# Opening of a stack of four graph attention layers: layer norm's scale moved to scores and V, row sums on VectorE, score rows by transposes, idle matmuls 20, 3 and 3

## The chip, the cores and the metric

The kernel runs on one core of a Trainium2 chip. The metric is the device time of one execution in microseconds (us), median over runs. Five engines work side by side, each through its own instruction list in order: TensorE (PE in the profile, with its weight loads as PEld), VectorE (DVE), ScalarE (ACT), GpSimd (POOL) and SyncE (SP); they wait for each other by semaphores. TensorE reads SBUF and writes PSUM. An fp32 matmul stands in the profile as two instructions, a transpose as one.

## What is computed

`x` is 2048 x 128 fp32, `adj` a 2048 x 2048 matrix of 0 and 1, some 0.8% ones. Four residual layers:

```python
h = jnp.maximum(_layernorm(x, axis=-1), 0.0)
x = x + _L0_gnn_ref(h, adj, W_heads, a1, a2, W_out, b_out)   # 8 heads, ELU, projection
h = jnp.maximum(_layernorm(x, axis=-1), 0.0)
x = x + _L1_gnn_ref(h, adj, W, r)                            # 1 head, exact GELU
...                                                          # two more, 1 head, ELU
# one head:
Wh = h @ W; s1 = Wh @ a1; s2 = Wh @ a2
e = leaky_relu(s1[:, None] + s2[None, :], 0.2)
att = softmax(where(adj > 0, e, NEG), axis=1)
hp = att @ Wh                                                # a row without a neighbour: the mean of Wh
```

The layer norm has no weights: `(x - m) / sqrt(v + eps)`. With y = 1 / sqrt(v + eps), one number per row and positive, relu((x - m) * y) is relu(x - m) * y.

## The kernel before

**Tiling.** The 2048 rows are 16 tiles of 128. A unit is one head and one half (`c`, 1024 output rows, 8 groups of 128). For each of 16 tiles `j` of source rows, VectorE makes a `probs` tile of 128 x 1024 in one scalar_tensor_tensor (L1183; in the first two tiles two halves of 512, L1180) out of `rho`, the row factors spread over the partitions, `t_now`, a column factor, and `adjT`, the transposed adjacency as 0 or 1 in bf16. TensorE multiplies the 8 blocks of it with `V[:, j, :]`, which holds 128 columns of W h times a factor v, and v itself as column 129, so that the last column gives the softmax's denominator (L447 in layer 0, L472 later). `probs` is a ring of 8 tiles. Layer 0 has 16 units: `unit(0, 0)` outside the loop, then a loop of 7 rounds with two units each, then the late layers with parts of 8, 6 and 2 groups.

**Opening.** SyncE loads X in two halves, then weights, then `adj` tiles into 7 landing places (5 in `stage`, one in `hpT`, one in `xn`); ScalarE casts each to bf16 (`cast`, L699), and a place is loaded again once it has been cast. Before the 7th, SyncE waits for the first two transposed blocks (L314), as `xn` then holds normed rows. VectorE takes mean and variance (L1090, L1094); ScalarE takes the inverse root (L705, L707), VectorE improves it by one Newton step (L1098 to L1101); both norm the 16 tiles (L1105, L714); TensorE transposes them in four blocks of 512 columns (L367), both engines copy them to `hT` with relu (L1110, L719, the latter with sums of rows). TensorE makes W h of head 0 and the s2 of all 8 heads in one product per tile (`first_wh_and_s2`, L378, 136 columns), then s1 of head 0 as rows for the first 1024 nodes (`s1`, L383, 2 matmuls of 512 columns), and, between these two, spreads the largest score over the partitions (`first_spread_max`, L404). From it follow the factors (L739, L740), V of tile 0 on VectorE (L1134) and of the others on ScalarE (`first_scale_v`), and `rho` (L752).

**Beside unit 0.** TensorE does asides between tiles: after j=1 the maxima of all heads (L411) and s1 of 8 heads for nodes 1024 to 2047 (`rows_of_heads(1)`, 2 matmuls of 512 columns, so 4 instructions), after j=7 the same for nodes 0 to 1023, after j=11 the mean of W h (`mean_rows`, L426). VectorE does `center_of_heads` after j=3, `mean` after j=6 (L1157 to L1163), `add_bias` after j=12 (L1252). ScalarE casts, scales V and makes `rho_rows`, which go through DRAM to `rho`.

**Loop.** In the odd unit `project` makes W h of the next head (L395), ScalarE's `scale_v` makes V of it (L759, L761) with `v_now`. After j=7 VectorE takes the denominators of the unit before, after j=8 it divides, after j=10 it makes the ELU and its 32 x 32 transposes; ScalarE moves the blocks (L796), and TensorE projects at j=10 or 11 (`aside`, L571).

**Idle matmuls.** `keep_warm(count)` issues matmuls of the identity whose result nobody reads (L416): 20 at the start, 2 + 2 after the score vectors (L586), `WARM_ROWS` = 8 in the transition from layer 1 to 2 (`rest_of_scores(1)`, L636), and `WARM_HOLE` = 4 at the end of each of the three transitions (L663), before the products of `late_unit(n, 0)`.

Of the kernel before, what the change touches and what calls it, by code (L numbers as in the profile page):

```python
# [14 lines left out]
def gat_stack(nc, x, adj_t, w0, w0_t, a0, w_out, b_out, w1_t, w1, r1, w2, w2_t, av2, w3, w3_t, av3, out):  # L15
# [7 lines left out]
    P = 128  # L23
# [20 lines left out]
    with ctx:  # L44
# [21 lines left out]
        s2_all = sb("s2_all", [P, NT, H])  # L66
# [8 lines left out]
        wa0 = sb("wa0", [P, 2, H])  # L75
# [35 lines left out]
        CT, CC, CW = 264, 396, 480  # L111
        FT, FC = 140, 270
# [4 lines left out]
        first_xn = [xn, rows[:, 0, :, :]]  # L117
# [12 lines left out]
        first_norm_dve = sem("first_norm_dve")  # L130
        first_norm_act = sem("first_norm_act")
# [169 lines left out]
        def _(sp):  # L301
# [59 lines left out]
        def _(pe):  # L361
            def transpose_first(r):

                pe.wait_ge(first_norm_dve, r + 1)
                pe.wait_ge(first_norm_act, r + 1)
# [5 lines left out]
            def first_wh_and_s2():  # L371
# [3 lines left out]
                for t in range(NT):  # L375
                    if t % 4 == 0:
                        pe.wait_ge(first_hT_act if t % 8 else first_hT_dve, t // 8 + 1)
# [205 lines left out]
            keep_warm(WARM_START[0], idle_first)  # L583
            pe.wait_ge(w0t_in, 32)
            for h in range(H):
                last = nc.tensor.matmul(score_bank[:, CW + 2 * h:CW + 2 * h + 2], W0t[:, h, :], a0_sb[:, h, :],  # L586
                                        start=True, stop=True)
            last.then_inc(wa_psum, 1)
# [104 lines left out]
        def _(act):  # L693
# [15 lines left out]
            def first_transposed():  # L709
                act.wait_ge(rstd_ready, 1)  # L710
                for r in range(4):
                    for k in range(2, 4):
                        at = 4 * r + k
                        last = nc.scalar.activation(first_xn[r // 2][:, at % NK, :], X[:, at, :], ACT.Identity,  # L714
                                                    bias=nwt[:, 3, at:at + 1], scale=nwt[:, 0, at:at + 1])
                    last.then_inc(first_norm_act, 1)
                for r in (1, 3):
                    act.wait_ge(first_hT_psum, r + 1)
                    nc.scalar.activation(hT[:, r * 512:(r + 1) * 512], first_banks[r], ACT.Relu,  # L719
                                         accum_out=hsum[:, r:r + 1]).then_inc(first_hT_act, 1)  # L720

            def first_copy_wh(b):

                act.wait_ge(first_wh, b + 1)
                ins = nc.scalar.activation(V[:, PER_BANK * b:PER_BANK * (b + 1), 0:D],
# [902 lines left out]
```

## Time and profile before

| | us |
|---|---|
| median of 3 runs | 758.48 (758.44 to 759.07) |
| the profiled execution, its own time | 759.12 |
| its span, first to last instruction | 757.4 |
| TensorE busy | 746.5 (99%) |
| VectorE busy | 619.6 (82%) |
| ScalarE busy | 326.4 (43%) |

The page's second part cuts the span in 40 slices of 18.9 us and gives the busy share of each in tenths:

```profile
PE   8999999999999999999999999999999999999997
DVE  4989679797787968879796797968788969898986
DMA  9993000000000000000000000000000000000001
```

TensorE is busy from end to end, a little less in the first slice; the transfers of `adj` fill the first three. A time of an instruction runs from its start to its end, and neighbours overlap, so for a rate the text takes the distance from one start to the next, or the chain of waits, which cuts the overlap off.

### The profile page before, as it was taken

To read this page: it belongs to the slowest core of one execution; us is meant where nothing else is said; L and a number is where in the kernel's file an instruction comes from. 1 tells how busy PE (TensorE), PEld (TensorE's weight loads), DVE (VectorE), ACT (ScalarE), POOL (GpSimd) and SP (SyncE) were. 2 spreads that over 40 slices of the span, in tenths; PEclk is the share of its full clock that TensorE was granted. 3 is DMA by queue.
4 is the path that set the end of the run, shared out by engine and by line. 5 is a ranking of instruction groups with operands and counts; after the bars stand their busy time and mean duration, and the time that the engine had idled before them with its cause. 6 is when DMAs were issued, how large, how long until landed. Compare 5 with 4: busy or idle time off the path is not lost.

```text
span 757.4 us, 16076 instructions
## 1 busy us (share of the span) xinstructions
PE 746.5 (99%) x6507; PEld 732.4 (97%) x6507; DVE 619.6 (82%) x1048; ACT 326.4 (43%) x878; POOL 16.6 (2%) x38
## 2 busy tenths in 40 slices
PE   8999999999999999999999999999999999999997
PEld 8789999999999999999999999999989989998997
DVE  4989679797787968879796797968788969898986
ACT  4978341452543346134353414534350352636230
POOL 3000000000000000000000000000000000000000
PEclk9999999999999999999999999999999999999999
DMA  9993000000000000000000000000000000000001
GB/s 293 341 373 109 29 29 1 28 0 28 28 0 28 0 28 0 28 28 0 28 0 28 28 0 28 0 0 1 2 2 1 1 1 2 1 1 1 2 26 32
DMA packets 13874, 29.39 MB, mean 39 GB/s; under 512 B 1296, under 2 KB 7568, under 8 KB 13840
## 3 DMA queue, kind: packets, MB, share of 16 engines
q1 hardware_dynamic: 11152, 20.00, 7.8%
q0 software_dynamic: 2688, 8.92, 3.4%
q8 instruction: 24, 0.39, 0.2%
q14 instruction: 10, 0.08, 0.0%
HBM read 27.80 MB, written 1.11 MB: 38 GB/s over the span
## 4 chain that ended last, share of the span: by engine, by line
PE 95%; DVE 3%; ACT 1%; DMA 1%; issue 0%; DVEq 0%; ACTq 0%
PE acc L447 57%; PE acc L472 26%; PE side L571 3%; PE side L395 3%; PE acc L524 1%; PE acc L416 1%; PE side L383 1%; DMA X<-in_x_dram 1%; PE side L535 1%; PE acc L378 0%; PE side L511 0%; DVE stats L1090 0%; PE side L497 0%; PE side L426 0%; PE side L367 0%
## 5 line engine op out<-in xcount | busy, mean ns | idle before, releaser
L447 PE MATMUL acc<-V,probs 128*128 128x129 f32 x3840 | 436.6, 275 | 1.5 <-DVE probs L1180 1.5
L447 PEld LDWEIGHTS acc<-V,probs 128*128 128x128 f32 x3840 | 432.6, 192 | 4.5 <-DVE V L1134 2.3
L1183 DVE SCALAR_TENSOR_TENSOR probs<-rho,t_now,adjT 128x1024 f32<-128x1024 f32 x238 | 290.0, 1277 | 13.9 <-PE acc L447 9.1
L1273 DVE SCALAR_TENSOR_TENSOR probs<-rho,t_now,adjT 128x768 f32<-128x768 f32 (+3 forms) x182 | 147.3, 868 | 13.3 <-PE acc L472 10.5
L796 ACT ACTIVATE hpT<-rows 32x256 f32<-32x256 f32 x224 | 92.8, 414 | 66.6 <-DVE rows L1220 64.2
L472 PE MATMUL acc<-stage,probs 128*128 128x129 f32 x1024 | 115.9, 275 | 0.0
L472 PEld LDWEIGHTS acc<-stage,probs 128*128 128x128 f32 x1024 | 115.0, 192 | 0.1
L472 PE MATMUL acc<-V,probs 128*128 128x129 f32 x768 | 89.4, 275 | 0.0
L472 PEld LDWEIGHTS acc<-V,probs 128*128 128x128 f32 x768 | 87.4, 192 | 0.1
L781 ACT ACTIVATE fill<-mean_now,empty 128x128 f32<-128x128 f32 x120 | 36.7, 396 | 89.8 <-DVE den L1196 89.8
L1228 DVE TENSOR_TENSOR X<-X,side 128x512 f32<-128x512 f32 x28 | 19.3, 688 | 65.9 <-PE side L571 65.9
L759 ACT ACTIVATE V<-v_now 128x4 f32<-128x4 f32 x28 | 5.9, 209 | 83.0 <-PE side L395 83.0
L761 ACT ACTIVATE V<-side,v_now 128x128 f32<-128x128 f32 x112 | 31.5, 363 | 0.0
L1205 DVE SCALAR_TENSOR_TENSOR rows<-acc,den,fill 128x128 f32<-128x128 f32 x112 | 30.8, 343 | 0.3
L395 PE MATMUL side<-W,hT 128*128 x224 | 29.6, 275 | 0.0
L571 PE MATMUL side<-Wout,hpT 128*128 x224 | 27.3, 275 | 0.0
L395 PEld LDWEIGHTS side<-W,hT 128*128 128x128 f32 x224 | 27.3, 192 | 0.0
L571 PEld LDWEIGHTS side<-Wout,hpT 128*128 128x128 f32 x224 | 26.1, 192 | 0.0
L893 ACT ACTIVATE rows<-acc,late_den 128x128 f32<-128x128 f32 x32 | 11.0, 394 | 30.5 <-DVE late_den L1311 26.3
L699 ACT ACTIVATE adjT<-stage 128x1024 bf16<-128x1024 int32 x24 | 23.8, 1043 | 0.0
L788 ACT ACTIVATE rows<-rows 128x512 f32<-128x512 f32 x28 | 17.5, 629 | 10.3 <-DVE rows L1205 10.2
L918 ACT ACTIVATE xn<-X,nwt 128x128 f32<-128x128 f32 x36 | 14.7, 482 | 16.6 <-DVE nwt L1415 16.6
(207 smaller groups left out, 406.5 us busy)
## 6 DMA issues: line engine op xcount, KB each, us to landing
stage<-in_adj_t_dram SPq DMA_DIRECT2D x24, 512.0 KB, 7.1
rho<-rho_dram POOLq DMA_DIRECT2D x15, 512.0 KB, 3.9
hpT<-in_adj_t_dram SPq DMA_DIRECT2D x4, 512.0 KB, 8.5
xn<-in_adj_t_dram SPq DMA_DIRECT2D x4, 512.0 KB, 7.2
X<-in_x_dram SPq DMA_DIRECT2D x2, 512.0 KB, 4.6
W0t<-in_W_t_dram SPq DMA_DIRECT2D x1, 512.0 KB, 5.2
W<-in_L_gnn_W_heads_dram SPq DMA_DIRECT2D x1, 512.0 KB, 6.5
Wout<-in_L_gnn_W_out_dram POOLq DMA_DIRECT2D x1, 512.0 KB, 10.2
```

The costliest lines, as they stand in the source:

```text
L395: last = nc.tensor.matmul(side[:, g % 2, k * D:(k + 1) * D], hT[:, j * P:(j + 1) * P], w, start=True, stop=True)
L447: last = nc.tensor.matmul(group(c, k), probs[:, j % RING, k * P:(k + 1) * P], V[:, j, :], start=(j == 0 and k % PER_BANK == 0), stop=(j == ...
L472: last = nc.tensor.matmul(group(c, k), slot_of(n, p, j)[:, i * P:(i + 1) * P], v[:, j, :], start=(j == 0 and k % PER_BANK == 0), stop=(j = ...
L571: last = nc.tensor.matmul(side[:, b, k * D:(k + 1) * D], hpT[:, 4 * b + k, :], w, start=True, stop=True)
L699: nc.scalar.activation(adjT[:, j, c * CH:(c + 1) * CH], landing(n), ACT.Sign).then_inc(adj_ready, 1)
L761: last = nc.scalar.activation(V[:, 4 * g + k, 0:D], side[:, g % 2, k * D:(k + 1) * D], ACT.Copy, scale=v_now[:, 4 * g + k:4 * g + k + 1])
L781: ins = nc.scalar.activation(fill[:, k, :], mean_now[:, :], ACT.Copy, scale=empty[:, c, k:k + 1])
L796: last = nc.scalar.activation(hpT[b:b + Q, :, a:a + Q], rows[a:a + Q, 1, :, b:b + Q], ACT.Copy)
L1183: nc.vector.scalar_tensor_tensor(probs[:, j % RING, :], rho[:, c * CH:(c + 1) * CH], t_now[:, j:j + 1], adjT[:, j, c * CH:(c + 1) * CH], A ...
L1205: ins = nc.vector.scalar_tensor_tensor(rows[:, 0, k, :], group(c, k)[:, 0:D], den[:, 3, k:k + 1], fill[:, k, :], ALU.mult, ALU.add)
L1228: nc.vector.tensor_tensor(at, at, side[:, b, :].rearrange("p (k d) -> p k d", k=4), ALU.add).then_inc(x_added, 1)
L1273: return nc.vector.scalar_tensor_tensor(slot_of(n, p, j)[:, first:end], rho[:, at + first:at + end], t_now[:, j:j + 1], adjT[:, j, at + fi ...
```

## The change

The centred rows relu(x - m) take the place of the normed ones. The scale y is put on later: on the scores as they leave PSUM (`first_scores_of`), and on V through `vy_now` and `vy_all`, v times y, while column 129 keeps v. So the first half is centred by ScalarE as soon as its means are there, the second by VectorE, and root and Newton step run behind the transposes. `W0s` is 144 columns wide and gives s1 of all heads too, by node in the partitions; rows of head 0 come from 8 matmuls of 128 columns against the identity, rows of all heads from 8 transposes per half. The sum of the rows of h is made on VectorE in unit 0 (`scale_of_rows` after j=5 and j=6 in place, `sum_of_rows` after j=7), a matmul with minus one brings it to the partitions, and ScalarE scales it. Score vectors are made in two groups of four heads with the first transposes between. The idle matmuls of 2 + 2 go, 8 become 3, 4 become 3. SyncE no longer waits ahead of the 7th load.

```diff
-    WARM_START, WARM_ROWS, WARM_HOLE = (20, 2), 8, 4
+    WARM_START, WARM_ROWS, WARM_HOLE = 20, 3, 3
-    MW = D + H
+    MW = D + 2 * H
...
-                elif n == SLOTS - 1:
-                    sp.wait_ge(first_hT_psum, 2)
...
-            def s1(k, wa_s1, bank):
-                nc.tensor.matmul(bank[0:wa_s1.shape[1], :], wa_s1, hT[:, k * 512:(k + 1) * 512],
-                                 start=True, stop=True).then_inc(s1_psum, 1)
+            def s1_of_first(tiles):
+
+                for t in tiles:
+                    last = nc.tensor.matmul(side[:, t // 4, (t % 4) * P:(t % 4 + 1) * P], s1_all[:, t, 0:1].to_broadcast([P, P]), ident[:, :],
+                                            start=True, stop=True)
+                if tiles[-1] % 4 == 3:
+                    last.then_inc(s1_psum, 1)
...
+            score_vectors(range(0, H // 2))
+            transpose_first(0)
+            score_vectors(range(H // 2, H))
+            for r in range(1, 4):
+                transpose_first(r)
...
-            keep_warm(WARM_START[1], idle_first)
-            wa1 = wa0[:, 0, :]
-            wa_head = wa0[:, 0, 0:1].to_broadcast([P, P])
-            keep_warm(WARM_START[1], idle_first)
-            for r in range(4):
-                transpose_first(r)
             first_wh_and_s2()
-            s1(0, wa_head, side[:, 0, :])
+            pe.wait_ge(scores_ready, 1)
+            s1_of_first((0, 1, 2, 3))
             first_spread_max()
-            s1(1, wa_head, side[:, 1, :])
+            s1_of_first((4, 5, 6, 7))
+            def sum_of_first():
+                pe.wait_ge(h_sum_ready, 1)
+                pe.wait_ge(rho_ready, 6)
+                nc.tensor.matmul(side[:, 0, 0:1], h_sum[:, :], minus_one[:, 0:1], start=True, stop=True).then_inc(h_sum_psum, 1)
 
             def rows_of_heads(c):
                 pe.wait_ge(rho_ready, 4 - 2 * c)
                 for k in range(2):
-                    s1(2 * c + k, wa1, side[:, k, :])
+                    for i in range(4):
+                        last = nc.tensor.transpose(side[0:H, k, i * P:(i + 1) * P], s1_all[:, 4 * (2 * c + k) + i, :], ident[:, :])
+                    last.then_inc(s1_psum, 1)
 
             unit(0, 0, 0, ((1, spread_max_of_heads), (1, lambda: rows_of_heads(1)), (7, lambda: rows_of_heads(0)),
-                           (11, lambda: mean_rows(1, W0[:, :, :].rearrange("p h d -> p (h d)"), H, rho_ready, 6)),
+                           (10, sum_of_first), (12, lambda: mean_rows(1, W0[:, :, :].rearrange("p h d -> p (h d)"), H, rho_ready, 6)),
                            ))
...
+            def first_centered():
+                act.wait_ge(neg_mean_ready, 1)
+                for t in range(NK):
+                    last = nc.scalar.activation(first_xn[0][:, t, :], X[:, t, :], ACT.Relu, bias=neg_mean[:, t:t + 1])
+                    if t % 4 == 3:
+                        last.then_inc(first_norm_act, 1)
...
+                nc.scalar.activation(vy_now[:, :], vy_all[:, bass.ds(h + 1, 1), :].rearrange("p a t -> p (a t)"),
+                                     ACT.Copy).then_inc(tv_ready, 1)
+                act.wait_ge(tv_ready, 2 * h + 4)
...
             nc.scalar.preload_act_table_set(LOG_EXP)
-            first_inverse_root()
+            first_centered()
+            first_transposed(0)
             act.wait_ge(wa_psum, 1)
             wa_scores = score_bank[:, CW:CW + 2 * H].rearrange("p (h s) -> p s h", s=2)
-            nc.scalar.activation(W0s[:, D:MW], wa_scores[:, 1, :], ACT.Copy)
-            nc.scalar.activation(wa0[:, :, :], wa_scores, ACT.Copy).then_inc(wa_ready, 1)
-            first_transposed()
+            nc.scalar.activation(W0s[:, D:D + H], wa_scores[:, 1, :], ACT.Copy)
+            nc.scalar.activation(W0s[:, D + H:MW], wa_scores[:, 0, :], ACT.Copy).then_inc(wa_ready, 1)
+            first_transposed(1)
+            first_inverse_root()
+            cast(0, 2)
             for b in range(NB):
-                if b < 2:
-                    cast(b, b + 1)
                 first_copy_wh(b)
-            cast(2, 3)
...
-            cast(15, 20)
+            cast(15, 17)
+            act.wait_ge(h_sum_psum, 1)
+            nc.scalar.activation(hmean[:, 1:2], side[:, 0, 0:1], ACT.Copy, scale=-1.0 / N).then_inc(hmean_ready, 1)
+            cast(17, 22)
...
+            def first_scores_of(t0, t1, raw):
+
+                y = nwt[:, 0, t0:t1]
+                to = scores_all[:, t0:t1, :]
...
+                    return nc.vector.tensor_tensor(to, raw, y, ALU.mult)
...
+                dve.wait_ge(first_vexp, 1)
+                nc.vector.tensor_tensor(vy_now[:, :], V[:, :, D], nwt[:, 0, :], ALU.mult).then_inc(first_vy, 1)
+                dve.wait_ge(first_vy, 1)
                 dve.wait_ge(first_copied, 1)
-                dve.wait_ge(first_vexp, 1)
-                nc.vector.tensor_scalar(V[:, 0, 0:D], V[:, 0, 0:D], V[:, 0, D:D + 1], None, ALU.mult).then_inc(first_v, 1)
+                nc.vector.tensor_scalar(V[:, 0, 0:D], V[:, 0, 0:D], vy_now[:, 0:1], None, ALU.mult).then_inc(first_v, 1)
...
+            def scale_of_rows(c):
+
+                own = first_xn[c]
+                y = nwt[:, 0, c * NK:(c + 1) * NK].rearrange("p (k d) -> p k d", d=1).to_broadcast([P, NK, D])
+                last = nc.vector.tensor_tensor(own, own, y, ALU.mult)
+                if c == 1:
+                    link(last)
+
+            def sum_of_rows():
+
+                nc.vector.tensor_reduce(h_sum[:, :], rows[:, :, :, :].rearrange("p c k d -> p d (c k)"), AX.X, ALU.add).then_inc(h_sum_ready, 1)
...
+            unit(0, 0, rho_and_adj(0, 0, True), ((3, center_of_heads), (5, lambda: scale_of_rows(0)), (6, lambda: scale_of_rows(1)),
+                                                     (7, sum_of_rows), (8, scale_of_heads), (12, add_bias)))
```

## Rows read from the trace of the kernel before

**Rows 1.** The page, part 1: busy us (share of the span) and instructions.

```profile
PE 746.5 (99%) x6507; PEld 732.4 (97%) x6507; DVE 619.6 (82%) x1048; ACT 326.4 (43%) x878; POOL 16.6 (2%) x38
```

**Rows 2.** The chain of waits, 0 to 60 us: start us, us, what.

```profile
7.20 1.53 DVE stats L1090 x8
...
13.82 1.71 PE acc L367 x8
15.53 3.78 PE acc L378 x32
19.31 0.86 PE side L383 x2
...
20.20 0.50 PE acc L404 x2
...
23.16 3.81 PE acc L447 x32
...
27.28 1.81 PE side L383 x4
```

**Rows 3.** The timeline of the opening: start us, us, engine, line, what.

```profile
8.81 1.95 PE L586 MATMUL acc<-a_sb,W0t 128*128 128x2 f32 x16 [0.71 <-DMA W0t<-in_W_t_dram]
...
22.06 0.29 DVE L1134 TENSOR_SCALAR V<-V 128x128 f32<-128x128 f32 x1 [0.49 <-ACT V L739]
22.26 2.74 DVE L1180 SCALAR_TENSOR_TENSOR probs<-rho,t_now,adjT 128x512 f32<-128x512 f32 x4
```

**Rows 4.** TensorE in stretches: A:B length, busy (count), granted clock, DMA share, GB/s.

```profile
8.73:12.14 3.41, 3.13 (x26) 1.00 1.10 367
12.14:15.55 3.41, 3.41 (x18) 0.50 1.04 356
...
18.96:22.37 3.41, 2.66 (x10) 1.00 1.03 382
```

**Rows 5.** VectorE's groups by shape: count, busy us, mean ns, idle before.

```profile
L1252 DVE TENSOR_TENSOR X<-X,bias_rep 128x2048 f32<-128x2048 f32 x1 | 2.3, 2284 | 0.0
...
L1427 DVE TENSOR_SCALAR xn<-X,mv 128x128 f32<-128x128 f32 x6 | 1.4, 283 | 0.1
...
L1457 DVE TENSOR_REDUCE neg_c<-acc 128x1 f32<-128x128 f32 x3 | 0.9, 291 | 1.5 <-PE acc L559 1.5
...
L1123 DVE TENSOR_REDUCE cmax<-s_all 128x8 f32<-128x128 f32 x1 | 0.4, 383 | 0.0
```

**Rows 6.** The timeline of units 0 and 1.

```profile
31.41 1.21 DVE L1157 TENSOR_REDUCE hsum<-hT 128x2 f32<-128x1024 f32 x1
...
32.92 3.67 DVE L1183 SCALAR_TENSOR_TENSOR probs<-rho,t_now,adjT 128x1024 f32<-128x1024 f32 x3
...
58.14 1.29 DVE L1183 SCALAR_TENSOR_TENSOR probs<-rho,t_now,adjT 128x1024 f32<-128x1024 f32 x1 [0.57 <-PE acc L447]
...
69.74 6.81 ACT L796 ACTIVATE hpT<-rows 32x256 f32<-32x256 f32 x16 [0.46 <-DVE rows L1220]
...
79.31 1.95 PE L571 MATMUL side<-Wout,hpT 128*128 x16
```

**Rows 7.** The chain of waits in the transition to layer 2.

```profile
546.56 1.88 PE acc L416 x16
...
548.66 0.44 PE side L511 x4
```

**Rows 8.** The timeline of the same transition.

```profile
546.60 1.26 ACT L918 ACTIVATE xn<-X,nwt 128x128 f32<-128x128 f32 x3
...
547.01 0.42 DVE L1342 SCALAR_TENSOR_TENSOR rows<-rows 128x256 f32<-128x256 f32 x1
...
556.06 3.93 DVE L1273 SCALAR_TENSOR_TENSOR probs<-rho,t_now,adjT 128x512 f32<-128x512 f32 x5 [0.42 <-ACT rho L959]
...
556.96 3.25 PE L472 MATMUL acc<-stage,probs 128*128 128x129 f32 x27
```

**Rows 9.** Waits of all engines: us in total, times, longest.

```profile
ACT V L759 <- PE side L395: 83.0, 28, 7.7
```

More of the change, by code:

```diff
@@ L116, in gat_stack @@
         first_banks = [side[:, 0, :], side[:, 1, :], acc[:, 1, 0, :], acc[:, 1, 1, :]]
-        first_xn = [xn, rows[:, 0, :, :]]
+        first_xn = [rows[:, 1, :, :], rows[:, 0, :, :]]
+        s2_all, s1_all = scores_all[:, :, 0:H], scores_all[:, :, H:2 * H]
         spare_bank, max_bank = acc[:, 0, 2, 0:2 * P], acc[:, 0, 2, 2 * P:3 * P]
@@ L362, in transpose_first @@
             def transpose_first(r):
-                pe.wait_ge(first_norm_dve, r + 1)
-                pe.wait_ge(first_norm_act, r + 1)
+                if r < 2:
+                    pe.wait_ge(first_norm_act, r + 1)
+                else:
+                    pe.wait_ge(first_norm_dve, r - 1)
                 for k in range(4):
@@ L582, in _, with score_vectors @@
             pe.wait_ge(ident_ready, 1)
-            keep_warm(WARM_START[0], idle_first)
+            keep_warm(WARM_START, idle_first)
             pe.wait_ge(w0t_in, 32)
[L585 to L588, printed above, removed]
+            def score_vectors(heads):
+                for h in heads:
+                    last = nc.tensor.matmul(score_bank[:, CW + 2 * h:CW + 2 * h + 2], W0t[:, h, :], a0_sb[:, h, :],
+                                            start=True, stop=True)
+                if heads[-1] == H - 1:
+                    last.then_inc(wa_psum, 1)
+            score_vectors(range(0, H // 2))
[3 more added lines that the diff above has]
+                transpose_first(r)
             def later_vectors():
@@ L707, in first_inverse_root, with first_transposed @@
                 nc.scalar.activation(nwt[:, 0, :], nwt[:, 2, :], ACT.Exp, scale=-0.5).then_inc(root_ready, 1)
[L709 to L720, printed above, removed]
+            def first_centered():
[4 more added lines that the diff above has]
+                        last.then_inc(first_norm_act, 1)
+            def first_transposed(r):
+                act.wait_ge(first_hT_psum, r + 1)
+                nc.scalar.activation(hT[:, r * 512:(r + 1) * 512], first_banks[r], ACT.Copy).then_inc(first_hT_act, 1)
             def first_copy_wh(b):
                 act.wait_ge(first_wh, b + 1)
+                act.wait_ge(scores_ready, 1)
                 ins = nc.scalar.activation(V[:, PER_BANK * b:PER_BANK * (b + 1), 0:D],
@@ L732, in first_scale_v @@
                     where = V[:, t, 0:D] if t < NK + 1 else first_group(t)[:, 0:D]
-                    last = nc.scalar.activation(V[:, t, 0:D], where, ACT.Copy, scale=V[:, t, D:D + 1])
+                    last = nc.scalar.activation(V[:, t, 0:D], where, ACT.Copy, scale=vy_now[:, t:t + 1])
                 last.then_inc(v_ready, 1)
@@ L829, in _ @@
             act.wait_ge(first_copied, NB)
-            act.wait_ge(first_vexp, 1)
+            act.wait_ge(first_vy, 1)
             first_scale_v(0)
-            cast(3, 6)
+            cast(2, 5)
             first_scale_v(1)
-            cast(6, 8)
+            cast(5, 8)
             factors()
@@ L1087, in first_norm @@
                 for c in range(2):
+                    own = slice(c * NK, (c + 1) * NK)
                     dve.wait_ge(x_in[c], 16)
@@ L1091, in first_norm @@
                     link(last)
-                    nc.vector.memset(nwt[:, 1, c * NK:(c + 1) * NK], 0.0)
                     for k in range(c * NK, (c + 1) * NK):
                         last = nc.vector.bn_aggr(mv[:, k, :], stats[:, k, :])
+                    if c == 0:
+                        link(last)
+                        nc.vector.tensor_scalar(neg_mean[:, :], mv[:, own, 0], -1.0, None, ALU.mult).then_inc(neg_mean_ready, 1)
                 last.then_inc(var_ready, 1)
-                y, s, m = (nwt[:, i, :] for i in (0, 1, 3))
+                dve.wait_ge(var_ready, 1)
+                for t in range(NK, NT):
+                    last = nc.vector.tensor_scalar(first_xn[1][:, t - NK, :], X[:, t, :], mv[:, t, 0:1], 0.0, ALU.subtract, ALU.max)
+                    if t % 4 == 3:
+                        last.then_inc(first_norm_dve, 1)
+                for r in (2, 3):
+                    dve.wait_ge(first_hT_psum, r + 1)
+                    nc.vector.tensor_copy(hT[:, r * 512:(r + 1) * 512], first_banks[r]).then_inc(first_hT_dve, 1)
+                y, s = (nwt[:, i, :] for i in (0, 1))
                 dve.wait_ge(root_ready, 1)
@@ L1140, in center_of_heads, with scale_of_heads @@
                 dve.wait_ge(rows_ready, 1)
-                s2 = s2_all[:, :, :].rearrange("p t h -> p h t")
+                s2 = s2_all.rearrange("p t h -> p h t")
                 nc.vector.tensor_tensor(d_all[:, :, :], s2, c_rep[:, :].rearrange("p (h t) -> p h t", t=1)
                                         .to_broadcast([P, H, NT]), ALU.subtract).then_inc(d_ready, 1)
+            def scale_of_rows(c):
[3 more added lines that the diff above has]
+                if c == 1:
+                    link(last)
+            def sum_of_rows():
+                nc.vector.tensor_reduce(h_sum[:, :], rows[:, :, :, :].rearrange("p c k d -> p d (c k)"), AX.X, ALU.add).then_inc(h_sum_ready, 1)
+            def scale_of_heads():
+                dve.wait_ge(tv_ready, 2)
+                nc.vector.tensor_tensor(vy_all[:, :, :], v_all[:, :, :], nwt[:, 0, :].rearrange("p (h t) -> p h t", h=1)
+                                        .to_broadcast([P, H, NT]), ALU.mult).then_inc(vy_all_ready, 1)
             def last_columns(to, c):
@@ L1254, in add_bias @@
                 dve.wait_ge(x_added, 1)
-            unit(0, 0, rho_and_adj(0, 0, True), ((3, center_of_heads), (6, lambda: mean(0, 1)), (12, add_bias)))
+            unit(0, 0, rho_and_adj(0, 0, True), ((3, center_of_heads), (5, lambda: scale_of_rows(0)), (6, lambda: scale_of_rows(1)),
+                                                     (7, sum_of_rows), (8, scale_of_heads), (12, add_bias)))
             dve.wait_ge(tv_ready, 2)
```

71 lines of the change are left out of this document (32 added, 39 removed).

## The prediction

> **What bounds the kernel now.** I read the page first: TensorE is busy for 746.5 of 757.4 us [rows 1]. So a change pays only where it takes instructions off TensorE, or where TensorE waits, and that is in the first 23 us and in the three transitions between late layers. Second, the chain of waits over the opening [rows 2]: it goes over VectorE's statistics, the transposes, 32 products of W h and s2 that end at 19.31, the spread of the maximum at 20.20, and the products of unit 0 from 23.16. From there it stays on TensorE, with `rows_of_heads` (1.81) inside. Third, the timeline of the opening [rows 3] and TensorE's granted clock [rows 4]: it is 0.50, the lower level of 1.2 GHz, from 12.14 to 15.55, after a stretch in which TensorE did 16 products of two columns, 8 idle matmuls and one or two transposes. Everything here is worked against the profiled execution, span 757.4, own time 759.12; that is 0.6 above the median of 758.48, and differences are taken over to the median as they are.
>
> **Opening, up to the products' end.** Removed: the wait of both norms for root and Newton step. Centring needs the means alone. Those of the first half are there when VectorE goes on to the second half, 7.20 [rows 2]; with a small negation and its links ScalarE starts at about 7.5. The nearest row for one step is 1.26 for three with scale and bias [rows 8], 0.42 each, so eight end by 10.9. VectorE begins its eight at about 9.7; the same form takes at most 0.283 [rows 5], so they end by 12.0. TensorE's score vectors start at 8.81 and take 1.95 [rows 3], four heads 0.98. Its list then: heads to 9.8, first block of transposes (0.44 at the high clock [rows 7]) to 10.2, heads to 11.2, second and third block to 12.1. Each finds its rows ready, by 0.2 us or more. The fourth block and the 32 products of W h follow. These widen from 136 to 144 columns: 3.78 / 32 = 0.118 [rows 2] becomes 0.125, altogether 0.2 more.
>
> Their clock is the open question. If it falls at 12.1 and comes back at 15.5, as before, a transpose costs 1.71 / 8 = 0.214 [rows 2] and a product 0.214 x 144 / 128 = 0.24. The fourth block ends at 12.9, eleven of the 32 run until 15.55, and the other 21 take 2.6: end at 18.2, 1.1 before the old 19.31. If it doesn't fall: 12.5 + 32 x 0.125 = 16.5, 2.8 before. I take the first. In the same stretch before, the idle matmuls gave 8 of 128 columns; the change gives 12 transposes and the same small products, and it drops the idle ones. That is little more than what let it fall.
>
> The Trainium skill, TensorE: Matmul & The Clock Gate, "Part 4: PE-mode transpose", says that transposes don't count as busy for the clock as matmuls do. The trace speaks against it, as the stretch from 12.14 to 15.55 held transposes almost alone and the clock rose at its end [rows 2, 4]. By that rule the case without a fall would be impossible, and the time that of the first case.
>
> **Opening, up to the first product.** From the end of the 32 to the spread it was 0.89 (19.31 to 20.20) with TensorE's s1 beside it (0.86) [rows 2]. Now the two last scaled reads and the same reduction stand there, and 8 instructions of 128 columns, 8 x 0.11 = 0.9: unchanged. The three copies to V (`first_copy_wh`), for which the spread waits, have the casts of two tiles before them; they end ahead of it in both cases. From the spread to the first product it was 2.96. Added: the product v times y on VectorE ahead of V of tile 0, with a wait on itself; the start-to-start distance of a small one is 0.20 [rows 3]. Queued behind it are V of tile 0 and the first probs half, for which TensorE waits. So +0.2, bounds 0.15 and 0.35. Root, Newton step and the two casts run behind transposes and W h: nothing. The opening gives 1.1 - 0.2 = 0.9.
>
> SyncE's removed wait starts the 7th load 5 us sooner, but the transfers are already at a share of 1.04 and more [rows 4] and land in turn: nothing. The cast of tile 2 moves behind the first scaling of V; VectorE wants it after four halves, 2.7 us [rows 3], and it is there after some 2.4. Cover 0.3 us, and TensorE doesn't want it before another 2 us.
>
> **Score rows.** 4 instructions in 1.81 [rows 2] become 8 transposes of 0.11, 0.9, twice: 1.8 to 1.9 off a busy TensorE. Their sum costs two instructions, 0.2 (bounds 0.1 and 0.4). Net 1.7.
>
> **VectorE in unit 0.** Each `scale_of_rows` is a tensor_tensor of 1024 elements: half of 2.28 [rows 5], with the fixed part 1.2; both 2.4. `scale_of_heads` adds 0.4. Removed are the old reductions, 31.41 to 32.92 [rows 6], 1.5. The reduction of 2048 elements reads them 512 bytes apart. No row shows that. Lower bound: contiguous, 2.28 [rows 5]. Above: 128 scores read 32 bytes apart took 0.383, 128 contiguous ones 0.291 [rows 5], so 0.72 ns more an element, 2.28 + 1.5 = 3.8. I take 3.8, the strided row being the nearer one.
>
> Who waits: probs tile 8 was ready at 32.92 + 2 x 1.22 = 35.4 [rows 6]; now 35.4 + 2.4 - 1.5 + 3.8 = 40.1. TensorE took it at 27.28 + 1.81 + 96 x 0.113 + 1.81 = 41.7 [rows 2], now 39.8. So 0.3 of waiting; with 2.28, none. The second place is the projection of unit 1. VectorE's tile 23 started at 58.14, and the moved blocks were ready 18.4 later at 76.55, TensorE projected at 79.31 [rows 6]. By its own work VectorE would reach tile 23 at 32.92 + 16 x 1.21 + 2.3 (bias) = 54.6; with 2.4 - 1.5 + 3.8 + 0.4 it is 59.7, and the blocks are ready at 78.1. TensorE comes at 79.31 - 1.7 + 0.3 = 77.9. So 0.2 more. Cost 0.4, bounds 0 and 0.6.
>
> ScalarE's row mean now waits for TensorE's sum, with 15 casts behind it. Its list is two casts past the last `rho_rows`, before the sum; the scaled mean is there some 3 us before `mean_rows`, which moved to j=12. Nothing; a late cast of tile 15 or 16 would put TensorE on wait from 3 us on. In the loop ScalarE makes one more copy of 16 columns per head, before `scale_v`; it waits there for TensorE 83.0 us over 28 times [rows 9]: nothing.
>
> **Idle matmuls.** Of `WARM_ROWS` 16 instructions took 1.88 [rows 7]; six take 0.7. What is late next is the norm: ScalarE's three end at 547.86, VectorE's ELU at 547.43 [rows 8]. So the four transposes start at about 548.0 and not 548.66 [rows 7], and ScalarE's and VectorE's chain behind them moves along: 0.65, bounds 0.4 and 0.8. `WARM_HOLE` gives nothing: the product starts 0.90 after the first probs half (556.06, 556.96 [rows 8]), exactly as in the opening, 22.26 to 23.16 [rows 2, 3], where no idle matmul stands between. So probs set it.
>
> **Sum.** 0.9 + 1.7 - 0.4 + 0.65 = 2.85, say 2.8: median 758.48 - 2.8 = 755.7, a span of 754.6.
>
> **Rivals.**
> - B, the clock stays high at 12.1: the 32 end at 16.5 and not 18.2, 1.7 more. 754.0. For it: more transposes in that stretch than before, and they seem to count. Against it: the idle matmuls are gone.
> - C, it falls as before and once more when the products of unit 0 start. From 18.96 to 22.37 TensorE was busy for 2.66 with four instructions of 512 columns among ten [rows 4]. Now this stretch holds some 1.3 us of 128 columns, not far above the one that let it fall. A stretch of 3.4 us at half rate costs 1.7: 757.4.
> - D, the other sign: the reduction over 512 bytes a step is dearer than the 32-byte row tells. TensorE's loss is its length less 3.4; the rest of the change gives 3.2. Slower by more than 1.5 from 8.1 us on, 4 ns an element; at 9 us it is 5.6 lost, 760.9. Against it: the row gives 1.9 ns an element.
> - E, the score rows are no cheaper: 8 stationary loads of other data in a row cost the 0.214 of the low clock each, and 1.8 goes: 757.5. Against it: 0.44 for four transposes [rows 7].
>
> **How the numbers follow.** 0.2% is about what a measurement of this kernel can tell from no change: 757.0 and 760.0 are the bounds. The likeliest case A has 42% (own range 755.0 to 756.6), B 27%, C 20%, D 5%, E 4%, anything else 2%. Faster by over 0.2%: nearly all of A and B and a quarter of C, 72%. Within: most of C, E and a rest of A, 22%. Slower: D and a rest, 6%. The range takes in B with its bounds and C: 753.6 to 757.8.
>
> **What would show it.** In the new trace: the 32 products end at 18.2 (A, C) or 16.5 (B); first probs product at 22.3 or 20.6; the granted clock 0.50 around 12 to 15.5 and, in C, after 22; the two groups of 8 transposes 0.9 each; `sum_of_rows` 3.8 (2.3, or above 8); one wait of TensorE of 0.3 at tile 8; TensorE at the four transposes after the shortened idle ones 0.65 sooner relative to its neighbours; `WARM_HOLE`'s product 0.90 after its probs. What would make it wrong: a ScalarE centring above 0.5 each, so that TensorE waits at the second block, or a clock that falls elsewhere.

## The result, and the profile after

| | before | changed |
|---|---|---|
| median, us | 758.48 (758.43 to 759.07, 5 runs) | 754.37 (754.28 to 755.99, 5 runs) |
| ratio | | 0.9947, 95% interval 0.9936 to 0.9959 |
| profiled execution, its span | 759.12, 757.4 | 754.51, 752.8 |

The changed kernel is 4.1 us faster, 0.5%. The forecast was 755.7 in a range of 753.6 to 757.8. What came is the rival B: TensorE's clock did not fall in the opening. Below, a "fall" is a stretch in which the granted clock is at its lower level, 0.50 (1.2 GHz), after it had been at 1.00 (2.4 GHz); the "mean clock" of an execution is its granted clock averaged over the whole span, so that a fall shows in it as 0.998 or less.

The page of the changed kernel, part 1:

```profile
PE 742.0 (99%) x6505; PEld 731.8 (97%) x6505; DVE 624.3 (83%) x1048; ACT 326.6 (43%) x884; POOL 16.6 (2%) x38
```

TensorE has 4.5 us less of busy time than in [rows 1], VectorE 4.7 more. The chain of waits of the changed kernel, 0 to 60 us (start, us, what), is to be set beside [rows 2]:

```profile
11.78 0.87 PE acc L377 x8
12.65 3.92 PE acc L388 x32
16.57 0.89 PE side L395 x8
...
17.46 0.50 PE acc L418 x2
...
37.46 5.60 PE acc L461 x48
43.06 0.12 PE side L627 x2
...
46.85 1.72 PE side L440 x4
```

The transposes (L377) take 0.11 each (0.87 for eight, before 1.71). The 32 products (L388; by count of instructions, they are 16 products of two each) end at 16.57, and the spread (L418) starts at 17.46 and not 20.20. The stretches of the same kernel, TensorE alone (A:B, length, busy, granted clock, DMA share, GB/s), to be set beside [rows 4]:

```profile
8.73:12.14 3.41, 3.41 (x34) 1.00 1.10 361
12.14:15.55 3.41, 3.41 (x30) 1.00 1.04 355
...
18.96:22.37 3.41, 1.82 (x16) 1.00 1.01 378
```

The granted clock is 1.00, the upper level, where it was 0.50. The timeline of units 0 and 1:

```profile
20.55 3.81 PE L461 MATMUL acc<-V,probs 128*128 128x129 f32 x32 [1.60 <-DVE probs L1230]
...
24.61 1.04 PE L633 MATMUL side<-ident,scores_all 128*8 128x128 f32 x8
...
32.38 3.75 DVE L1196 TENSOR_REDUCE h_sum<-rows 128x128 f32<-128x2048 f32 x1
...
37.46 5.60 PE L461 MATMUL acc<-V,probs 128*128 128x129 f32 x48 [0.22 <-DVE probs L1233]
```

The first product starts at 20.55 (before 23.16). The eight transposes that make score rows take 1.04, the end of the last one included, and VectorE's reduction 3.75. TensorE waits 0.22 for probs tile 8. The projection of unit 1 stands in the chain as

```profile
75.37 1.99 PE side L585 x16
```

In the transition to layer 2 the chain of waits reads:

```profile
538.71 2.23 PE acc L486 x20
540.95 0.88 PE acc L549 x2
...
543.68 0.41 PE acc L503 x2
544.11 0.63 PE side L525 x4
...
549.37 0.49 PE acc L573 x2
```

The shortened idle group (`WARM_ROWS`) is off this chain altogether: the transposes (L503) wait for VectorE's ELU now, which ends at 543.54, and those of L525 stand behind them.

### The profile page after: what moved, and what is told of

The parts are those of the page before. It is cut to its first block, busy times and chain, and to the rows that moved or that the text cites. A ratio compares the mean times of both kernels' runs of the same rounds, so it can differ in the third digit from the quotient of the medians.

```text
span 752.8 us, 16085 instructions
## 1 busy us (share of the span) xinstructions
PE 742.0 (99%) x6505; PEld 731.8 (97%) x6505; DVE 624.3 (83%) x1048; ACT 326.6 (43%) x884; POOL 16.6 (2%) x38
## 4 chain that ended last, share of the span: by engine, by line
PE 94%; ACT 3%; DVE 2%; issue 1%; POOL 0%; POOLq 0%; DVEq 0%
PE acc L461 55%; PE acc L486 26%; PE side L585 3%; PE side L409 3%; ACT adjT L723 1%; PE acc L430 1%; PE acc L538 1%; ACT V L756 1%; PE acc L388 1%; PE side L549 1%; PE side L525 0%; PE side L511 0%; PE side L440 0%; DVE stats L1431 0%; ACT xn L947 0%
## 5 line engine op out<-in xcount | busy, mean ns | idle before, releaser
L461 PE MATMUL acc<-V,probs 128*128 128x129 f32 x3840 | 436.7, 275 | 1.8 <-DVE probs L1230 1.6
L461 PEld LDWEIGHTS acc<-V,probs 128*128 128x128 f32 x3840 | 432.6, 192 | 2.7 <-DVE V L1175 1.8
L486 PE MATMUL acc<-stage,probs 128*128 128x129 f32 x1024 | 115.9, 275 | 0.2
L486 PEld LDWEIGHTS acc<-stage,probs 128*128 128x128 f32 x1024 | 115.0, 192 | 0.6 <-issue 0.6
L486 PE MATMUL acc<-V,probs 128*128 128x129 f32 x768 | 89.4, 275 | 0.1
L486 PEld LDWEIGHTS acc<-V,probs 128*128 128x128 f32 x768 | 87.4, 192 | 0.3 <-issue 0.3
L784 ACT ACTIVATE V<-side,vy_now 128x128 f32<-128x128 f32 x112 | 31.5, 363 | 0.0
```

The source lines that it names most:

```text
L461: last = nc.tensor.matmul(group(c, k), probs[:, j % RING, k * P:(k + 1) * P], V[:, j, :], start=(j == 0 and k % PER_BANK == 0), stop=(j == ...
L486: last = nc.tensor.matmul(group(c, k), slot_of(n, p, j)[:, i * P:(i + 1) * P], v[:, j, :], start=(j == 0 and k % PER_BANK == 0), stop=(j = ...
L784: last = nc.scalar.activation(V[:, 4 * g + k, 0:D], side[:, g % 2, k * D:(k + 1) * D], ACT.Copy, scale=vy_now[:, 4 * g + k:4 * g + k + 1])
```

## Experiments

The line numbers of the changed kernel: products of the units L461 and L486, transposes of the opening L377, the 32 products L388, the spread L418, the spread of layer 2 L573, idle matmuls L430, the rows of all heads L633. All differences between kernels below are of medians, and within the traces of starts in the chain of waits.

**a_same: the changed kernel again.** No edit.

> The changed kernel once more, to see in how many executions the clock falls in the opening and what it costs: expected one in five with a mean clock of 0.996 to 0.998, 1.6 to 1.8 us above the others, which lie at 754.3 to 754.6. A rival by which the difference of the two levels is not the clock would show the levels without a difference in the clock.

The times are 754.17 to 754.28 in five runs, the mean clock 0.999 or 1.0 in each; ratio to before 0.9940 (0.9926 to 0.9953). None had a fall, so the longer time of a fall didn't show here. It did in the first five (755.99 at a mean clock of 0.996; the others 754.28 to 754.51 at 0.999 or 1.0), and in the next run.

**a_idle_8_4: idle matmuls of the late transitions back.**

```diff
-    WARM_START, WARM_ROWS, WARM_HOLE = 20, 3, 3
+    WARM_START, WARM_ROWS, WARM_HOLE = 20, 8, 4
```

> The changed kernel with the idle matmuls of the late transitions back at 8 and 4. Theory: 0.65 to 0.8 us more at the transition to layer 2, where the transposes wait behind them, and nothing at the other two, where the probs set the start: 755.1. Rival 1: the fourth one of the three transitions counts too, 0.22 each, 755.7. Rival 2: fewer idle matmuls cost clock, so putting them back gains: under 754.3.

The median is 755.02, 0.65 to 0.8 above the changed kernel's 754.37 and 754.23. One of its four executions had a fall; the other three, at 754.79, 754.94 and 755.10, are 0.6 to 0.7 above. By the chain, the transition from the products' end to the spread:

```profile
542.43 1.72 PE acc L549 x4
544.15 1.88 PE acc L430 x16
...
551.53 0.49 PE acc L573 x2
```

From the first to the last of these starts it is 9.10; in the changed kernel, from 540.95 to 549.37, 8.42. The 16 idle instructions are on the chain again, and the difference of 0.68 is all of it. At the end of the transition the timeline shows the start of the first probs half and of the product:

```profile
553.65 2.74 DVE L1324 SCALAR_TENSOR_TENSOR probs<-rho,t_now,adjT 128x512 f32<-128x512 f32 x4 [0.42 <-ACT rho L988]
...
554.54 1.69 PE L486 MATMUL acc<-stage,probs 128*128 128x129 f32 x13
```

They are 0.89 apart with four idle ones and 0.90 with three (551.48 and 552.38), so the fourth is free. Both rivals are refuted.

Its profiled execution, 756.72, is one in which the clock fell in the opening, and the instructions of the opening are those of the changed kernel. The stretch and the chain:

```profile
11.80:15.20 3.40, 3.40 (x17) 0.52 1.04 354
```

```profile
11.75 1.69 PE acc L377 x8
13.43 4.78 PE acc L388 x32
...
19.10 0.50 PE acc L418 x2
```

That is case A: the 32 products end at 18.21, and the spread is at 19.10, 1.64 after the changed kernel's 17.46. So one and the same opening runs either way.

**a_start10: ten idle matmuls fewer at the start.**

```diff
-    WARM_START, WARM_ROWS, WARM_HOLE = 20, 3, 3
+    WARM_START, WARM_ROWS, WARM_HOLE = 10, 3, 3
```

> The changed kernel with 10 and not 20 idle matmuls at the start. Theory (the clock carries the opening): TensorE has nothing from about 6 us until the weights land at 8.8, the granted clock falls or stays low through score vectors, transposes and part of the 32 products, and the first product of unit 0 comes 1.5 to 3 us later, 756 to 757.5. Rival (the order of the work carries it, the clock is a small matter): the idle matmuls reached past the landing at 8.9, so without them the opening is 0.3 sooner, 754.1.

The median is 758.69 (757.25 to 759.14, 10 runs): the whole gain is gone by ten matmuls that nobody reads. Stretches and chain of its profile:

```profile
8.80:12.00 3.20, 3.20 (x17) 0.50 1.09 365
12.00:16.00 4.00, 4.00 (x20) 0.50 1.05 358
16.00:20.00 4.00, 4.00 (x23) 0.65 1.02 347
```

```profile
8.62 1.87 PE acc L602 x8
...
13.89 1.71 PE acc L377 x8
15.60 5.57 PE acc L388 x32
```

TensorE idles for 2.8 us ahead of the weights. Then score vectors, transposes and some 13 of the 32 products run at the low level (the 32 take 5.57 and not 3.92, at 0.12 more for each that is slow), and the first product comes at 25.15, 4.6 later. In this profile the theory holds, and its 1.5 to 3 us were too few: I had not counted the score vectors (1.87 and 1.5 for 0.79 twice) and had the clock back too soon. The ten executions are not all of this kind: five have a mean clock of 0.992 or 0.993 (758.7 to 759.1), three 0.995 (757.3 to 757.5), and two have 0.999 and still take 758.5 and 758.7. No profile of such a one was kept, so what made those two long is open.

**b_idle_12 and b_idle_0: the kernel before with more and with no idle matmuls ahead of its transposes.**

```diff
-    WARM_START, WARM_ROWS, WARM_HOLE = (20, 2), 8, 4
+    WARM_START, WARM_ROWS, WARM_HOLE = (20, 6), 8, 4
```

> The kernel before with 6 + 6 and not 2 + 2 idle matmuls between score vectors and transposes, 1.8 us more of work that nobody reads, of which 0.2 lies in a wait. Theory (where the clock falls, the transposes and some products pay for it): no execution has the low clock at the transposes, mean clock 0.999 or 1.0 in all of them; against the executions that kept the clock it is 1.6 slower, 760.0, against those in which it fell 1.0 slower. Rival (idle work is free there, since norms and not TensorE set the transposes): 758.4.

The median is 758.84 against 758.55 of before beside it. Eight of ten executions kept the clock (758.70 to 758.97), two did not (760.3 and 760.4). So 1.8 us more of idle work cost 0.4 against those of before that kept it (758.31 to 758.67), not 1.6. Both expectations are wrong, mine by taking TensorE to be on the path there for all of it. Against the profile of b_same below, in which the norms hold the transposes, the last transposes end at 15.26 and not 14.89 and the first product comes at 22.89 and not 22.51: of the 1.8, the 0.4 by which the idle work reaches past the norms.

```diff
-    WARM_START, WARM_ROWS, WARM_HOLE = (20, 2), 8, 4
+    WARM_START, WARM_ROWS, WARM_HOLE = (20, 0), 8, 4
```

> The kernel before without the 2 + 2 idle matmuls. Theory: TensorE waits for the norms there, so no time by itself; but with less work ahead of the transposes the clock falls in more executions, so more of them at the upper of the two levels 758.4 and 759.1, and perhaps a longer low clock. Rival (these idle matmuls are without effect): half the executions at either level, as before.

The median is 759.23: one execution of ten kept the clock (758.39), four are at 758.9 to 759.0 and five at 759.4 to 759.7. Its profile, one of the five, has the 32 products in 4.62 and the spread at 20.74. The idle matmuls that the change drops did serve the clock of the kernel before, in which 31 of 48 executions kept it.

**b_same: the kernel before, a second profile.**

> The kernel before once more, for a second profile. If its clock stays high in the opening (expected in 6 of 10), its transposes take 0.9 and not 1.7 to 1.9 per eight, but the spread of the maximum is only 0.6 sooner than 20.2, since the last normed rows of ScalarE (14.1) hold the fourth block either way. A rival, by which the two levels 758.4 and 759.0 lie elsewhere in the kernel, would show the spread at 20.2 and the 0.6 later on.

This execution took 758.48, with the clock kept. Its timeline:

```profile
12.46 1.65 ACT L714 ACTIVATE rows<-X,nwt 128x128 f32<-128x128 f32 x4
...
13.44 0.42 PEld L367 LDWEIGHTS acc<-ident,rows 128*128 128x128 f32 x4 [0.34 <-DVE rows L1105]
13.47 1.40 PE L367 MATMUL acc<-ident,rows 128*128 128x128 f32 x8
...
19.55 0.49 PE L404 MATMUL acc<-ident_neg,cmax 128*128 128x128 f32 x2
```

The last eight transposes take 1.40, not 0.87, with 0.34 of waiting for rows between, and ScalarE's last normed row ends at 14.1. The spread is at 19.55, 0.65 before 20.20, and the first product at 22.51 and not 23.16. So in the kernel before the norms cover most of a fall: it costs 0.6. Further down its chain stand `mean_rows` in unit 0, which ends at 50.24, and the transition to layer 2:

```profile
48.52 1.72 PE side L426 x4
...
541.97 2.23 PE acc L472 x20
...
553.30 0.49 PE acc L559 x2
```

In the 48 runs of before beside the experiments, 17 have a mean clock of 0.997 and, but for one at 760.2, lie at 758.8 to 759.2; the others have 0.999 or 1.0 and lie at 758.2 to 758.8.

**a_root_first: the root ahead of the centring.**

```diff
             nc.scalar.preload_act_table_set(LOG_EXP)
+            first_inverse_root()
             first_centered()
             first_transposed(0)
...
             first_transposed(1)
-            first_inverse_root()
```

> The changed kernel with ScalarE's inverse root ahead of its centring again, so that the first half's rows wait for the variances of both halves, as the norm did before, 9.6 us and not 7.4. Theory (the early centring is what feeds TensorE through the opening): the first block of transposes comes at about 11.8 and not 9.9, the spread of the maximum 1.9 to 2.2 us later than 17.4, and where the clock falls in the wait some more; 756.2 to 757.5. Rival (the order of TensorE's list and the removed scale are the gain, ScalarE has time): within 0.5 of 754.3.

The median is 757.61 (755.9 to 759.26, 10 runs), and the times stand in three groups: three executions at 755.9 (mean clock 1.0), four at 757.6 to 757.7 (0.996 to 0.998), three at 759.2 to 759.3 (0.994). The profile is of the first group; timeline and chain:

```profile
11.32 0.66 PE L377 MATMUL side<-ident,rows 128*128 128x128 f32 x4 [1.33 <-ACT rows L736]
```

```profile
18.94 0.50 PE acc L418 x2
```

TensorE waits 1.33 for the rows, and the spread is 1.5 late where 1.9 to 2.2 were expected. 755.9 is 1.6 above the changed kernel, so the rival is refuted. The groups are 1.7 and 1.6 apart, about what one fall costs, and the lower mean clocks fit one and two falls. No profile of the second or third group was kept, so where in the kernel they lie is not shown, and they don't show rival C.

**a_rows_mm: the score rows by products again.**

```diff
-                    for i in range(4):
-                        last = nc.tensor.transpose(side[0:H, k, i * P:(i + 1) * P], s1_all[:, 4 * (2 * c + k) + i, :], ident[:, :])
-                    last.then_inc(s1_psum, 1)
+                    nc.tensor.matmul(side[0:H, k, :], W0s[:, D + H:MW], hT[:, (2 * c + k) * 512:(2 * c + k + 1) * 512],
+                                     start=True, stop=True).then_inc(s1_psum, 1)
```

> The changed kernel with one part undone: the score rows of all heads come from two products of 512 columns per half again and not from 8 transposes (they are taken without the layer norm's scale, so the values of the rows differ). Theory (TensorE is busy there, so its instructions are paid in full): 4 instructions of 0.45 in place of 8 of 0.11 at either place, 0.9 to 0.95 more each, 1.8 to 1.9 us in all, 756.2. Rival (eight stationary loads of other data cost as much as the wide products): within 0.3 us of the changed kernel, 754.4.

The median is 755.77, 1.4 to 1.5 above the changed kernel where 1.8 to 1.9 were expected, ratio to before 0.9960. The chain:

```profile
20.31 3.81 PE acc L461 x32
...
24.44 1.81 PE side L632 x4
26.25 10.92 PE acc L461 x96
```

The four instructions take 1.81 in place of 0.97, and again 1.81 in place of 0.87 at the second place (both in a_contig's chain, where TensorE doesn't wait either): 0.84 and 0.94, 1.8 in all. The products behind them start slower too: the 96 behind the first place take 10.92 and not 10.72, the 48 behind the second 5.56 and not 5.36, which is 0.4 more. At the first place it sits in the first seven, which take 0.98; the first seven of a_contig take 0.78. From the first product to the end of `mean_rows` it is 29.74 against a_contig's 27.56, so the score rows are worth 2.2, and the medians of these two runs are 2.1 apart. The changed kernel shows only 1.4 to 1.5 of it, because there TensorE waits for VectorE at tile 8 and at the projection of unit 1; with the dearer score rows it comes later and waits at neither (the projection takes 1.79 and not 1.99). The two are one account: the transposes give 2.2, and VectorE takes 0.7 of it back.

**a_contig: the reduction over neighbours.**

```diff
-                nc.vector.tensor_reduce(h_sum[:, :], rows[:, :, :, :].rearrange("p c k d -> p d (c k)"), AX.X, ALU.add).then_inc(h_sum_ready, 1)
+                nc.vector.tensor_reduce(h_sum[:, :], rows[:, :, :, :].rearrange("p c k d -> p (c k d)").rearrange("p (a b) -> p a b", b=2 * NK), AX.X, ALU.add).then_inc(h_sum_ready, 1)
```

> The changed kernel with the reduction of h reading its 2048 elements one behind the other and not 512 bytes apart (so it sums other elements than the rows' sum; the mean row is not the reference's). Theory (the distance is what makes it 3.75 us, and its length makes TensorE wait at probs tile 8 and at the projection of unit 1): 2.2 to 2.4 us, both waits of 0.2 gone, 754.0. Rival (128 results instead of one make it long): 3.75 as before and 754.4.

The median is 753.65, 0.6 to 0.7 below the changed kernel. The sum of other elements is a wrong mean row, so this kernel is only for measuring. Its timeline and its chain:

```profile
32.49 2.28 DVE L1196 TENSOR_REDUCE h_sum<-rows 128x128 f32<-128x2048 f32 x1
...
34.68 1.27 DVE L1233 SCALAR_TENSOR_TENSOR probs<-rho,t_now,adjT 128x1024 f32<-128x1024 f32 x1
```

```profile
25.75 10.72 PE acc L461 x96
36.47 0.87 PE side L633 x8
37.35 5.36 PE acc L461 x48
...
75.02 1.79 PE side L585 x16
```

The reduction takes 2.28 with the same 128 results, so the distance between elements makes the other 1.47. It is also what tile 8 waits for: the chain of the changed kernel names ScalarE's cast, which ends at 36.03 beside the reduction, but here `probs` of tile 8 starts at 34.68, before that cast ends (36.13). The three tiles from tile 8 on take 5.36 on the chain and not 5.60. From the first product (20.66) to the end of `mean_rows` (48.22) it is 27.56, in the changed kernel 28.02, and the projection itself is 1.79 and not 1.99: 0.46 + 0.2 = 0.66.

**best: the sum by halves, V of tile 0 by two factors.**

```diff
-                nc.vector.tensor_tensor(vy_now[:, :], V[:, :, D], nwt[:, 0, :], ALU.mult).then_inc(first_vy, 1)
-                dve.wait_ge(first_vy, 1)
                 dve.wait_ge(first_copied, 1)
-                nc.vector.tensor_scalar(V[:, 0, 0:D], V[:, 0, 0:D], vy_now[:, 0:1], None, ALU.mult).then_inc(first_v, 1)
+                nc.vector.tensor_scalar(V[:, 0, 0:D], V[:, 0, 0:D], V[:, 0, D:D + 1], nwt[:, 0, 0:1], ALU.mult, ALU.mult).then_inc(first_v, 1)
+                nc.vector.tensor_tensor(vy_now[:, :], V[:, :, D], nwt[:, 0, :], ALU.mult).then_inc(first_vy, 1)
...
-                nc.vector.tensor_reduce(h_sum[:, :], rows[:, :, :, :].rearrange("p c k d -> p d (c k)"), AX.X, ALU.add).then_inc(h_sum_ready, 1)
+                link(nc.vector.tensor_tensor(rows[:, 0, :, :], rows[:, 0, :, :], rows[:, 1, :, :], ALU.add))
+                link(nc.vector.tensor_tensor(rows[:, 0, 0:4, :], rows[:, 0, 0:4, :], rows[:, 0, 4:8, :], ALU.add))
+                link(nc.vector.tensor_tensor(rows[:, 0, 0:2, :], rows[:, 0, 0:2, :], rows[:, 0, 2:4, :], ALU.add))
+                nc.vector.tensor_tensor(h_sum[:, :], rows[:, 0, 0, :], rows[:, 0, 1, :], ALU.add).then_inc(h_sum_ready, 1)
```

> The changed kernel with two mends. The row sum is made by four additions of halves (1024, 512, 256 and 128 elements, all neighbours) and not by one reduction over 512 bytes a step; and V of tile 0 takes both factors, v and y, in one instruction, with their product for the other tiles behind it. Theory: VectorE's 3.75 us become 1.2 + 0.7 + 0.4 + 0.3 = 2.6, both waits of TensorE of 0.2 (probs tile 8, projection of unit 1) go with what hangs on them, 0.7 in all as with the reduction over neighbours, and the first product comes 0.2 sooner: 753.5. Rival (the three added waits of VectorE on itself and a slower two-factor form eat it): 754.0 or more.

The median is 753.79 (753.64 to 755.03, 5 runs), ratio to before 0.9937 (0.9924 to 0.9951), against 754.23 of the changed kernel beside it. It is 0.4 faster, and the four executions with the clock kept (753.64 to 753.85) lie below all of the changed kernel's. From the first product to the projection of unit 1 it has a_contig's 54.36. The second mend gave little. Timeline of VectorE:

```profile
19.11 0.34 DVE L1173 TENSOR_SCALAR V<-V,nwt 128x128 f32<-128x128 f32 x1 [0.42 <-ACT V L762]
19.37 0.17 DVE L1174 TENSOR_TENSOR vy_now<-V,nwt 128x16 f32<-128x16 f32 x1
19.46 2.73 DVE L1232 SCALAR_TENSOR_TENSOR probs<-rho,t_now,adjT 128x512 f32<-128x512 f32 x4
```

From the spread to the first product it is 3.02 (17.33 to 20.35) and was 3.09. The small product (L1174) still stands ahead of the probs, and V now takes 0.26 from start to start. So the second mend gave 0.07 and not 0.2.

## Why the prediction was right, and where it wasn't

The mechanisms held, the case that I held likeliest did not come, and the rival that did gave 754.0 for 754.37. The range held because it was made to take in that rival; the number 755.7 itself was the wrong case.

**The clock, the step that failed.** "I take the first" was wrong in three ways. First, how often: with this opening it fell in 3 of 28 executions (the changed kernel, a_same, a_idle_8_4, a_rows_mm, a_contig, best), in the kernel before in 17 of 48. Second, the reason I gave: that 12 transposes in place of 8 instructions of idle matmuls were little more than what let it fall. It was enough to keep the clock in most executions. Third, I compared a forecast with a fall to a median without one. The profiled 759.12 is an execution with a fall; the median is not. With a fall on both sides the change gives 759.0 - 756.0 = 3.0 (I had 2.8), without one 758.4 - 754.3 = 4.1. The difference is the finding of this case: before, the norms covered most of a fall, now TensorE alone sets the opening up to the spread, and a fall costs 1.64 by the traces (1.3 to 1.8 by the times) where it cost 0.6. The 1.7 of the forecast is right for the changed kernel. Rival B's 754.0 has the same flaw: its 4.5 is worked against the profile with a fall, and there it holds (spans 757.4 to 752.8, 4.6), but the median before is 0.6 lower.

Why the clock falls in one execution of a kernel and not in another is not shown. The moment at which the instructions first become fast differs: the 40 idle instructions at the start took 6.46 in the first profile of before and 7.42 in the second, 7.57 in the changed kernel's. Where they end early, TensorE waits for the weights. It waited 1.05 in a_idle_8_4, the only profile of this opening with a fall, and 0.71 (a_same), 0.27 (a_rows_mm), 0.16 (best) or not at all (the changed kernel, a_contig) in those without. One profile with a fall is a hint and no proof, and a_root_first waited 1.33 for its rows and kept the clock. That the work ahead of the stretch matters is shown by b_idle_0, b_idle_12 and a_start10; a_root_first, where that work stands behind a wait, points the same way by its mean clocks.

**Transposes and the clock.** [rows 2, 4] spoke against the rule of the Trainium skill, TensorE: Matmul & The Clock Gate, "Part 4: PE-mode transpose", that transposes don't count as busy for the clock. Case B, which has no place under that rule, came in 25 of 28 executions, with transposes where the idle matmuls had been; with neither ahead of it, in b_idle_0, the clock fell in nine of ten.

**Opening.** The working for B said 16.5 for the end of the 32 products and 20.6 for the first product; the trace has 16.57 and 20.55. For A it said 18.2 and, for the spread, 19.1; a_idle_8_4 has 18.21 and 19.10. The stretch from the spread to the first product grew from 2.96 to 3.09, by 0.13 where I had 0.2. The landing of the weights and the later rise moved the start of the score vectors between 8.7 and 9.3 in the profiles, a term I didn't have. Without a fall on either side the opening gave 22.51 - 20.55 = 1.96. That the early centring carries most of it is shown by a_root_first, 1.5 at the spread; the rest, with the new order of TensorE's list and of the casts, no run takes apart.

**Score rows.** The forecast counted the instructions alone, 1.8 to 1.9, and those gave 1.8; rival E is refuted. With the 0.4 at the start of the products behind them they are worth 2.2; why these start slower is not shown. The sum cost 0.12 and as much again in the 32 products behind it (3.68, where 32 take 3.57 elsewhere), the 0.2 of the forecast. So the term of 1.7 was 1.9 to 2.0.

**VectorE in unit 0.** The reduction took 3.75 for 3.8, as the strided row said and not the contiguous one; TensorE lost 0.22 at tile 8 for 0.3, and 0.2 at the projection for 0.2. Taken away, it gave 0.66 in a_contig, more than my 0.4 and its bound of 0.6: the wait at tile 8 is put at 0.22, but the stretch around it is 0.46 longer. This miss and that of the score rows cancel, which is luck: from the first product to the end of `mean_rows` the forecast had 1.7 - 0.3 = 1.4, and the traces have 1.50. Rival D, from 8.1 us on, is refuted. ScalarE's mean was there at 43.4, with `mean_rows` at 46.7, 3.3 ahead.

**Idle matmuls.** They gave 0.68 for 0.65 in the transition to layer 2, and nothing where I had nothing, by a_idle_8_4.

The account of spans without a fall goes from 756.8 (b_same) to 752.8, 4.0 in all. The opening gives 1.96; from the first product to the end of `mean_rows`, with tile 12 counted on both sides (1.79; the changed kernel has it ahead of `mean_rows`), 50.24 + 1.79 - 22.51 = 29.52 to 48.57 - 20.55 = 28.02, 1.50; the wait at the projection takes 0.2 back; the transition to layer 2, from its last run of products to the spread, 553.30 - 541.97 = 11.33 to 549.37 - 538.71 = 10.66, 0.67. The sum is 3.93.

## What to carry to other kernels

Before a forecast is set against a median, see which clock the profiled execution had and whether the median had the same; their mean clocks tell it in most cases (not in two executions of a_start10). When a change takes the cover of other engines off TensorE, a fall of its clock that was nearly free is paid in full, and idle matmuls ahead of it change their value: ten of them were worth 4.3 us here. Instructions of TensorE can be worth more than their own time, and a wait elsewhere can hide part of it: compare two runs in which TensorE doesn't wait to see the whole price. And a reduction that is cheap by its count is not if its elements lie far apart; adding one half to the other four times, over neighbours, did it in some 2.6 us for 3.75.

## What the runs showed of the hardware

- VectorE's reduction of 2048 fp32 elements per partition takes 2.28 us over neighbours and 3.75 over elements 512 bytes apart, 0.72 ns more for each. The 128 elements 32 bytes apart of [rows 5] had given the same 0.72, though against a contiguous row that reads PSUM.
- A TensorE that is busy by the profile can lose its clock: in the kernel before it was busy for 3.13 of 3.41 us [rows 4] ahead of the fall, 16 of 26 instructions being of two columns. (They are 8 products of two instructions each, and the 8 idle instructions are 4 matmuls; the prediction gives both counts as if each were a product of its own.)
- An fp32 transpose of 128 columns costs half of an fp32 product of 128 columns, 0.11 to 0.22, with a stationary side of 128 or of 8 columns.
- Behind the four score row instructions of 512 columns (8 stationary columns), 96 instructions of the products take 10.92, behind the eight transposes 10.72. Behind the four instructions of `mean_rows`, of 512 columns too but with 128 stationary ones, there is no such loss (103 in 11.50).
- The same kernel has times in groups: 755.9, 757.6 and 759.2 in a_root_first, 1.7 and 1.6 apart, at mean clocks of 1.0, 0.996 to 0.998 and 0.994.
- The granted clock of the profile doesn't tell the level at the start. In a_start10 the first 20 idle instructions took 4.17, 0.21 each, with a granted clock of 1.00 in the trace; in [rows 7] 16 took 1.88, 0.12 each.
